# Layer 0 loop of a four-layer graph network on one core: order of score and raising products on TensorE

## What is computed

```python
S1 = jnp.einsum('id,kdh->ikh', Q, A1)            # Q, K, V = atoms @ W + b
S2 = jnp.einsum('jd,kdh->jkh', K, A2)
kidx = jnp.clip(edges, 0, nb - 1)                # edges = adj, so 0 or 1
e = S1[rows[:, None], kidx] + S2[rows[None, :], kidx]
e = jnp.where(valid, jax.nn.leaky_relu(e, negative_slope=0.2), 0.0)
attn = jax.nn.softmax(e, axis=1)                 # 8 heads
out = jnp.einsum('ijh,jhd->ihd', attn, Vh).reshape(n, h * d)
return out @ Pw + Pb
```

## Time and profile before

| | us |
|---|---|
| median of 3 runs | 1007.69 |
| lowest, highest | 1005.52, 1007.92 |
| the profiled execution | 1009.88 |
| its span | 1007.8 |

### The profile page before, as it was taken

One profiled execution on the slowest core, in us unless ns is written; L12 is line 12 of the kernel. 1 busy time (PEld: TensorE's weight loads), 2 busy tenths in 40 slices (PEclk: granted clock), 3 DMA queues, 4 the chain that ended last, 5 costly groups with the idle time before them and its releaser, 6 DMA issues.

```text
span 1007.8 us, 17904 instructions
## 1 busy us (share of the span) xinstructions
PE 899.0 (89%) x6926; PEld 326.3 (32%) x6926; DVE 730.0 (72%) x1170; ACT 563.1 (56%) x977; POOL 559.7 (56%) x674
## 2 busy tenths in 40 slices
PE   6899999999999999999996498999769489999960
PEld 6733222222222222222224322333323245554420
DVE  3656558887878887888885697123469659999987
ACT  2689666666666666666661284001120358899960
POOL 3266569889898998889880100000000028899952
PEclk9979999999999999999998599999869867999985
DMA  9571111211212121120000000000000000000000
GB/s 172 136 138 34 53 59 40 71 35 31 68 35 71 36 64 41 27 78 24 24 23 1 1 1 1 1 1 2 1 1 1 1 0 1 1 0 1 1 0 21
DMA packets 23034, 32.63 MB, mean 32 GB/s; under 512 B 14587, under 2 KB 14715, under 8 KB 21926
## 3 DMA queue, kind: packets, MB, share of 16 engines
q1 hardware_dynamic: 20646, 23.11, 8.0%
q0 software_dynamic: 2304, 8.39, 4.6%
HBM read 38.58 MB, written 1.29 MB: 40 GB/s over the span
## 4 chain that ended last, share of the span: by engine, by line
PE 73%; DVE 18%; issue 5%; ACT 3%; SPq 0%; DMA 0%; POOL 0%; DVEq 0%; ACTq 0%
PE ps L1240 23%; PE ps L1250 11%; PE ps L1388 8%; PE ps L1227 6%; DVE big L467 5%; PE ps L1219 4%; PE ps L1413 3%; PE ps L1336 3%; PE ps L1449 2%; DVE big L815 2%; DVE big L464 2%; PE ps L1096 2%; PE ps L1421 1%; PE ps L1207 1%; DVE big L601 1%
## 5 line engine op out<-in xcount | busy, mean ns | idle before, releaser
L601 DVE COPY_PREDICATED big<-mask,ps 128x512 f32<-128x512 uint8 x512 | 341.7, 730 | 113.6 <-PE ps L1227 109.6
L410 POOL TENSOR_SCALAR big<-big 128x512 f32<-128x512 f32 x512 | 355.6, 711 | 74.3 <-PE ps L1250 72.3
L963 ACT ACTIVATE ps<-ps 128x512 f32<-128x512 f32 x512 | 268.7, 583 | 141.7 <-PE ps L1219 141.4
L1240 PE MATMUL ps<-big 128*32 128x512 f32 x2048 | 253.6, 600 | 0.0
L436 POOL TENSOR_TENSOR big<-big 128x512 f32<-128x512 f32 x40 | 67.4, 1684 | 263.8 <-ACT big L1046 263.8
L1250 PE MATMUL ps<-big 128*32 128x512 f32 x1024 | 134.5, 597 | 0.0
L1219 PE MATMUL ps<-op_r,op_l 18*128 18x512 bf16 x512 | 111.7, 384 | 3.9 <-DVE big L601 2.2
L1240 PEld LDWEIGHTS ps<-big 128*32 128x32 f32 x2048 | 53.7, 109 | 119.7 <-issue 110.3
L1449 PE MATMUL ps<-big 66*128 66x512 f32 x160 | 86.3, 669 | 2.2 <-DVE big L788 1.3
L1227 PE MATMUL ps<-op_r,op_l 9*128 9x512 bf16 x512 | 74.7, 388 | 0.5 <-ACT ps L963 0.3
L467 DVE TENSOR_TENSOR big<-big,mask 128x512 f32<-128x512 f32 (+1 forms) x72 | 65.8, 933 | 5.4 <-ACT big L988 3.6
(11 more groups left out here) (277 smaller groups left out, 1110.0 us busy)
## 6 DMA issues: line engine op xcount, KB each, us to landing
big<-max_scratch SPq DMA_DIRECT2D x8, 1024.0 KB, 4.8
big<-rden_scratch SPq DMA_DIRECT2D x30, 256.0 KB, 3.3
big<-in_adj_dram POOLq DMA_DIRECT2D x12, 512.0 KB, 8.9
op_l<-split_scratch SPq DMA_DIRECT2D x56, 36.0 KB
op_r<-split_scratch SPq DMA_DIRECT2D x56, 36.0 KB
work<-in_adj_dram POOLq DMA_DIRECT2D x2, 512.0 KB, 13.1
h_nat<-in_adj_dram POOLq DMA_DIRECT2D x2, 512.0 KB, 12.0
x_nat<-in_x_dram SPq DMA_DIRECT2D x1, 512.0 KB, 4.6
```

The source lines that it names most:

```text
L410: pool.tensor_scalar(ring[:, k % RING, :], vrow[:, head % 2, i0:i0 + HALF], HUGE, g0[:, head, jt:jt + 1], ALU.min, ALU.max).then_inc(s["ba ...
L601: dve.copy_predicated(ring[:, k % RING, :], mask[:, jt, i0:i0 + HALF], ps[:, slot("tile", k), :])\
L963: act.activation(ps[:, at_slot, :], ps[:, at_slot, :], ACT.Relu, scale=-1.0).then_inc(s["relus"], 1)
L1240: m = pe.matmul(ps[32 * w:32 * (w + 1), MAIN, :], vp[:, head, jt + w // 2, 32 * (w % 2):32 * (w % 2 + 1)], ring[:, (u + w // 2) % RING, :] ...
```

## The change

In each visit the items of visit v are issued first, and the raising products of visit v - 1 behind them. The units stay last. The other engines' streams are as they were. The diff:

```diff
             pe.wait_ge(s["vp_read"], BLOCKS)
             for v in range(LAST):
-                for kind, k in trio(v - 1):
-                    if kind == "tile":
-                        raise_floor(k)
                 for kind, k in trio(v):
                     if kind == "tile":
                         cross(k)
                     elif kind == "adj":
                         turn_adj(k, free_slot("adj", k))
                     else:
                         values(k)
+                for kind, k in trio(v - 1):
+                    if kind == "tile":
+                        raise_floor(k)
                 for u in range(units(v), units(v + 1)):
                     if u % 3 < 2:
                         aggregate(4 * (u // 3) + 2 * (u % 3))
```

## The result

| | before | after |
|---|---|---|
| median us | 1007.81 (4 runs, 1005.52 to 1011.24) | 1060.05 (4 runs, 1058.74 to 1060.62) |
| ratio, 95% interval | | 1.0509 [1.0485, 1.0533] |
| the profiled execution | 1009.88 | 1058.74 |
| its span | 1007.8 | 1056.6 |

The kernel is 5.1% slower, 52.2 us between the medians. The forecast was 1061.6 in 1044 to 1080.

The account below looks back on a forecast made before the run. TensorE was taken as the bound, with VectorE just in time. 27.9 + 11.0 + 9.8 + 5.2 = +53.9 us took the profiled execution from 1009.88 to 1063.8, 2.2 over the median, hence 1061.6, range 1044 to 1080.

Parts of the forecast that it names:

- Steady part: Three-tile visits from visit 40: the third score product waits for VectorE, four visits take 11.14 instead of 10.42; +27.9 us in all.
- The 2.53 rule: Three-tile visits: the third score product may go 0.49 + 1.98 + 0.06 = 2.53 us after the previous visit's first raise.
- The size of what VectorE does besides: Three-tile visits: of VectorE's additions and denominator reductions, 1.5 us shows in each 16 visits, making them 46.1.
- the 4.1 carried over from before: Three-tile visits: VectorE's additions (1.01 each) and denominator reductions (0.43) take 4.1 us in 16 visits.
- Adjacency and value visits: Visits 6 to 39: transposes or value product delay raises; pairs take 5.87 (+11.0 us in all) and 6.42 (+9.8).
- The start: First six visits, at a clock of 0.53 of full: +5.2 us, or about +3 at the full clock.
- 3.4 a visit: First six visits at the low clock: rounds, transposes, selects and release take 3.4 us a visit, three of them to 62.1.
- 3.65 more as today: End of the first six visits: 3.65 us follow the transposes at 62.6, as from 57.96 to 61.61 before.
- The rival of the late raise beside the third cross: Three-tile visits: a raise always goes one round behind a delayed third cross; +13 us more, 1075; 12%.
- The clock: Rival for visits 6 to 23: short gaps make TensorE's clock fall; +32 us, 1093; 4%.
- The faster rival: The raises' weight loads truly wait 108.7 us for ScalarE, and crosses ahead fill up to 58 us: 950; 1%.
- Only the extra rounds count: Rival: waits are hidden; 0.33 in each of 34 visits is +11, some +15 with the first visits: 1023; 4%.

Follow-up runs that it names:

- half selects: VectorE's select (line 601) cut to 256 of 512 columns of each tile: 1015.52 us on the changed kernel, 997.16 us on the kernel before.
- the third kernel: Changed kernel, but in the first 40 visits the adjacency or value item goes behind the raises (products of line 1227): 1032.62 us, ratio 1.0236.
- two crosses ahead: Kernel before, but in three-tile visits two score products (line 1219) precede the three products of line 1227 and the third follows: 1018.44 us, ratio 1.0102.
- the first raise second: Kernel before, but three-tile visits go cross (line 1219), raise (line 1227), cross, raise, raise, cross: 1008.93 us, ratio 1.0013.
- the kernel where GpSimd was idle beside it: Changed kernel with GpSimd writing only 256 of 512 columns of each ring buffer from tile 16 on: 1057.40 us, ratio 1.0497.

## Why the prediction was right, point by point

- **Steady part, right.** The visits were to be 3.25, 2.75, 2.53 and 2.61, sum 11.14; they are 3.25, 2.75, 2.58 and 2.58, sum 11.16. The 2.53 rule holds in its parts: raise to select 0.52 (354.21, 354.73), or 0.70 where no cross is late (348.88, 349.58), three selects 1.99, release to weights 0.05. The 0.52, where 0.49 was carried over, is most of why the third visit takes 2.58 and not 2.53. The half selects show that this release makes 22.6 of the 24.9 (24.9 - 2.3).
- **The size of what VectorE does besides: off.** Sixteen visits came to 45.8 (412.10 / 9) where 46.1 stood: of VectorE's work besides the selects 1.2 shows (45.8 - 44.6), not 1.5, and nine times 0.3 are the 3 us missed. The term that was mis-sized is the 4.1 carried over from before. In after the 26 additions have a median of 0.68 instead of 1.01, so with three of them there is about 1 us less to show; that this is the cause is argued, not tried. Placed elsewhere, VectorE's other work gave back 10 us, about the 9 x 1.2 that showed, and the three-tile visits of that kernel take 401.8 us, 44.6 in sixteen: the four visits of the rule and nothing besides.
- **Adjacency and value visits, right.** A pair with transposes lasts 5.82 (108.21 to 114.03, second cross to second cross), one with a value product 51.15 / 8 = 6.39, where 5.87 and 6.42 were worked out. Transposes 0.32 behind the cross, raises 0.55 behind those, select 0.49 behind the raise, as carried over. That the item is to blame and not the crosses is shown by the third kernel.
- **The start: mis-sized.** +7.4, in a range of some 5.7 to 7.7 over all profiles, where +5.2 stood. The term "3.4 a visit" left out that a raise's own round is longer at the low clock: the select comes 0.71 behind it (53.11, 53.82), not 0.49, and the visit takes 3.60 (53.11 to 56.71). With that and a later first wait, visit 5's transposes stand 15.6 behind the first cross (59.34), not 14.3. And "3.65 more as today" took over a stretch in which the clock was already rising; now visit 5's two units are at the low clock to their end, 3.64 long (60.84), and visit 6 begins 5.1 behind the transposes, not 4.2.
- **The rival of the late raise beside the third cross: false in its place.** A raise beside a late cross gave its select in 0.52 (354.21, 354.73). Its mechanism is real, though, one step elsewhere: with two crosses ahead the first raise did give its result a round late, and 11 us hung on it.
- **The clock: false.** It was 1.00 from 66 to 592 us with short gaps in most visits, and stayed 1.00 where the rule of the Trainium skill named in the prediction ("TensorE: Matmul & The Clock Gate") would have had it swing between its levels.
- **The faster rival: false, as argued.** The 108.7 us behind ScalarE went to 8.5 and nothing was gained; they were the units' stream.
- **Only the extra rounds count: false, but it is the rest.** With half selects the change costs 17.1, near the 15 that this rival gave.

## What to carry to other kernels

Before moving a product ahead of others, find who hands back its buffer and when, and compare that with the moment at which the product now wants to go: 0.08 us to spare in a two-unit visit turned into waits of up to 0.36, and these into 24.9 of the 52.9 us. The rest came from an item put between two groups that had run side by side. An in-order engine that waits at the head of a group also starves the engine that it waits for, here VectorE, whose next input stood behind the waiting cross. And a busy share (VectorE 72%) tells nothing of this: cutting its selects in half gained 1% in the one order and 4% in the other.

## What the runs showed of the hardware

- **A product whose strip is taken is issued, and ends later.** Up to four small products were in the array at once in different strips of 32 rows (three raises and a cross, 351.94 and 351.95). One in a taken strip is shown with a start at once, and its result comes a round (0.22) later (raise to select 0.71 with two crosses ahead, 0.53 with the first raise second). A product behind it in a free strip goes ahead: the third cross, which needs the second raise's strip, still started 0.23 behind it (384.62, 384.84). A start in the timeline is thus no proof that the product runs; its consumer tells.
- **An addition of VectorE's can be held for microseconds.** The same 128 x 512 addition took from 0.62 to 4.41 us in one kernel and up to 5.96 in another, 0.67 each time in the kernel where GpSimd was idle beside it, and the four held ones ended 0.54 after GpSimd's unbroken work did. The selects beside the same writes kept their 0.66. The Trainium skill ("GPSIMD Engine Reference", 8. Key points) says that GpSimd shares its SBUF interfaces with VectorE and contends with VectorE instructions that have two SBUF inputs, as this addition has; by that rule, the trace agrees, and gives the size.
